# Row-sum reciprocals through a small DRAM tile, the first residual's constant folded, and the key stacking begun by ScalarE

## What is computed

```
x = L0(x)   1x1 conv to q, k, v (128 channels); per channel softmax(q k^T) v over the 32 x 32 image;
            1x1 conv back; y * inv + (beta - mean * inv); + x
x = L1(x)   group norm (32 groups); qkv; 8 heads of 32 channels over 1024 tokens:
            softmax(q^T k) v; projection + b_proj; + x
x = L2(x)   group norm (16); k, v; softmax of k over channels and over tokens; context = k v^T;
            out = context^T q; group norm; exact gelu; 1x1 conv; + the normalised input
x = L3(x)   + bias; separable FIR up by 2; leaky relu * sqrt 2; separable FIR down by 2
```

## Time and profile before

| what | us |
|---|---|
| median of 3 runs (lowest, highest) | 4347.69 (4339.87, 4350.91) |
| the profiled execution | 4343.08 |
| its span, first to last instruction | 4341.1 |
| TensorE (PE) busy | 3821.6 |
| VectorE (DVE) busy | 2956.3 |
| ScalarE (ACT) busy | 2988.7 |
| GpSimd (POOL) busy | 41.4 |

### The profile page before, as it was taken

The page is one execution under the profiler, slowest core; times in us unless marked ns, Lnnn a source line. Parts: engine busy times, 40 slices in busy tenths (PEclk is TensorE's granted clock), DMA queues, the critical chain, the costliest instruction groups (busy, mean ns, idle before and its releaser), DMA issues.

```text
span 4341.1 us, 73525 instructions
## 1 busy us (share of the span) xinstructions
PE 3821.6 (88%) x22913; PEld 1888.4 (44%) x22913; DVE 2956.3 (68%) x5147; ACT 2988.7 (69%) x6992; POOL 41.4 (1%) x57
## 2 busy tenths in 40 slices
PE   4989899898988989898898988989898998989876
PEld 2445445353453535445353443535445353444422
DVE  3666767677767776677677767767676677767653
ACT  1877677777777777667777767777667777767831
POOL 0000000000000000000000000000000000000000
PEclk7889999999999999999999999999999999989886
DMA  2111120111111011120111112011121111211000
GB/s 68 49 30 50 30 60 8 42 42 35 55 31 50 11 35 55 30 60 18 39 35 35 55 30 60 2 40 50 30 60 27 29 35 35 55 30 49 1 10 10
DMA packets 65221, 160.17 MB, mean 37 GB/s; under 512 B 15088, under 2 KB 16752, under 8 KB 62736
## 3 DMA queue, kind: packets, MB, share of 16 engines
q1 hardware_dynamic: 64784, 154.71, 13.5%
HBM read 19.91 MB, written 16.78 MB: 8 GB/s over the span
## 4 chain that ended last, share of the span: by engine, by line
PE 56%; DVE 17%; issue 14%; ACT 11%; SPq 1%; DVEq 1%; ACTq 0%; DMA 0%; POOL 0%; POOLq 0%
PE ps L1056 21%; PE ps L1129 8%; PE ps L1084 7%; PE ps L1100 7%; DVE mxh L640 6%; ACT ps L950 4%; PE ps L1518 3%; ACT prob L941 2%; DVE st L525 2%; PE ps L1550 2%; PE ps L1568 2%; PE ps L1577 1%; ACT u L1012 1%; PE ps L1116 1%; PE ps L1465 1%
## 5 line engine op out<-in xcount | busy, mean ns | idle before, releaser
L950 ACT ACTIVATE ps<-ps,mxh 128x512 f32<-128x512 f32 x2048 | 1369.8, 678 | 467.5 <-DVE mxh L640 441.2
L640 DVE TENSOR_REDUCE mxh<-ps 128x1 f32<-128x512 f32 x2048 | 1311.9, 681 | 343.7 <-PE ps L1100 335.7
L941 ACT ACTIVATE prob<-ps 128x512 f32<-128x512 f32 x2048 | 1128.1, 615 | 510.8 <-PE ps L1084 507.6
L1084 PE MATMUL ps<-qs,ks 97*128 97x512 f32 x2048 | 920.1, 528 | 90.5 <-ACT prob L941 63.3
L1100 PE MATMUL ps<-ks,qs 96*128 96x512 f32 x2048 | 740.2, 431 | 109.2 <-ACT ps L950 87.5
L1084 PEld LDWEIGHTS ps<-qs,ks 97*128 97x128 f32 x2048 | 365.8, 198 | 600.1 <-issue 372.1
L1129 PE MATMUL ps<-prob,vo 128*32 128x512 f32 x4096 | 584.0, 644 | 0.0
L1100 PEld LDWEIGHTS ps<-ks,qs 96*128 96x128 f32 x2048 | 411.6, 201 | 293.2 <-ACT ps L950 188.5
L950 ACT ACTIVATION_READ_ACCUMULATOR ps<-ps,mxh 128x1 f32 x2048 | 448.9, 219 | 0.0
L1056 PE MATMUL ps<-xn,wqk 128*128 128x512 f32 x512 | 266.8, 652 | 3.7 <-DVE xn L564 3.7
L1056 PE MATMUL ps<-wkv,xn 128*128 128x512 f32 x512 | 242.7, 608 | 19.3 <-DVE xn L564 18.4
(11 more groups left out here) (123 smaller groups left out, 3868.8 us busy)
## 6 DMA issues: line engine op xcount, KB each, us to landing
qs<-hi SPq DMA_DIRECT2D x256, 128.0 KB, 2.3
ks<-hi SPq DMA_DIRECT2D x256, 128.0 KB, 2.3
xb<-in_x SPq DMA_DIRECT2D x32, 512.0 KB, 4.2
qs<-lo SPq DMA_DIRECT2D x128, 128.0 KB, 2.3
ks<-lo SPq DMA_DIRECT2D x128, 128.0 KB, 2.3
xa<-xb SPq DMA_DIRECT2D x16, 1024.0 KB, 4.7
out<-xn SPq DMA_DIRECT2D x32, 512.0 KB, 2.6
qs<-mrow SPq DMA_DIRECT2D x64, 8.0 KB, 1.8
```

Source lines behind the costliest of these rows:

```text
L640: dve.tensor_reduce(mxh[:, k, e:e + 1], ps[:, MAX_BANKS[at % 3], :], AX_X, ALU.max, negate=True).then_inc(max_ok.sem, 1)
L941: act.activation(prob[:, n % 2, h, :], ps[:, k % 2, :], ACT.Exp).then_inc(p_ok.sem, 1)
L950: act.activation(ps[:, bank, :], ps[:, bank, :], ACT.Exp, bias=mxh[:, k, e:e + 1], accum_out=sumh[:, m // NT % 2, k, e:e + 1]).then_inc(su ...
L1084: pe.matmul(ps[:, k % 2, :], ks[0:STACK + 1, (u // 2) * Q4 + h, s * P:(s + 1) * P], qs[0:STACK + 1, u, h, :], start=True, stop=True).then_ ...
```

## The change

Three parts. First, `spread`, `pick`, `mrow` and `reciprocals_in` on VectorE go. VectorE copies only the 32 rows to `srow`; SyncE sends the lower 16 rows to a DRAM tile of 4 x 512 floats (in the slot of `turnN`, ahead of `rows_in`, which now reads srow) and, in the slot of `rowsN`, reads it back with a broadcast of each head's row to 32 partitions, into `recs`. Before it overwrites srow, VectorE waits for the store of the unit before and for the `normalise` before that. Second, xb keeps L0's residual without its constant; the mean of L1's first norm gets `add0` added before the averaging and subtracted again for the bias, and `b_proj` takes it up for the later residual. Third, the 12 transfers of each key stack are issued by ScalarE, behind its sums in the slots of v0a (ahead of gelu) and v1a; the query stacks stay with SyncE at q0b and q1b. `BANK` and `bank_free` are written anew for the entries that are left.

```diff
@@ SyncE
-            def stack(b, before, g, part):
+            def stack(b, before, g):
-                sp.wait_ge(hi1_ok.sem, hi1_ok(b, 2 * (2 * g + part + 1)))
-                sp.wait_ge(lo1_ok.sem, lo1_ok(b, 2 * (2 * g + part + 1)))
+                sp.wait_ge(hi1_ok.sem, hi1_ok(b, 4 * g + 2))
+                sp.wait_ge(lo1_ok.sem, lo1_ok(b, 4 * g + 2))
...
+            def reciprocals_out(b, t):
+                sp.wait_ge(row_ok.sem, row_ok(b, t + 1))
+                sp.wait_ge(recs_in.sem, recs_in(b, t - 1))
+                sp.dma_start(recd.rearrange("h (t n) -> (h t) n", n=P), srow[4 * Q4:8 * Q4, :])\
+                    .then_inc(recd_in.sem, 16)
+            def reciprocals_in(b, t):
+                sp.wait_ge(recd_in.sem, recd_in(b, t))
+                sp.dma_start(recs[:, :], recd.unsqueeze(1).to_broadcast([Q4, DH, HALF])).then_inc(recs_in.sem, 16)
@@ VectorE
+                if n == 0:
+                    step(dve.tensor_tensor(mv[:, n, :, 0], mv[:, n, :, 0], add0[:, :], ALU.add))
+                    last()
...
+                if n == 0:
+                    step(dve.tensor_tensor(gm[:, n, :, 0], gm[:, n, :, 0], add0[:, :], ALU.subtract))
+                    last()
...
-                if hf == 1:
-                    dve.wait_ge(res0.sem, res0(j, 2 * ct + 2))
-                    dve.tensor_scalar(xb[:, ct, :], xb[:, ct, :], add0[:, ct:ct + 1], None, ALU.add).then_inc(x1_ok.sem, 1)
...
+                if t:
+                    dve.wait_ge(recd_in.sem, recd_in(b, t - 1))
+                    dve.wait_ge(att_ok.sem, att_ok(b, t - 1))
                 bank = BANK[f"turn{t}"] if t else 6
-                dve.tensor_copy(mrow[:, :], ps[0:4 * Q4, bank, 0:P]).then_inc(row_ok.sem, 1)
                 dve.tensor_copy(srow[:, :], ps[0:8 * Q4, bank, 0:P]).then_inc(row_ok.sem, 1)
-            def reciprocals_in(b, u):
-                dve.wait_ge(spread_mm.sem, spread_mm(b, u + 1))
-                dve.wait_ge(att_ok.sem, att_ok(b, u))
-                dve.tensor_copy(recs[:, :], ps[:, BANK[f"rows{u + 1}"], :]).then_inc(spread_ok.sem, 1)
@@ ScalarE
+            def stack_keys(b, before, g):
+                act.wait_ge(lo1_ok.sem, lo1_ok(b, 4 * g + 4))
+                act.wait_ge(hi1_ok.sem, hi1_ok(b, 4 * g + 4))
+                if before is not None:
+                    act.wait_ge(s_mm.sem, s_mm(before, STEPS * Q4 // 2 * (g + 1)))
+                for h in range(Q4):
+                    for r, of in enumerate((hi1, hi1, lo1)):
+                        act.dma_start(ks[DH * r:DH * r + DH, g * Q4 + h, :].bitcast(F32),
+                                      of[DH * h:DH * h + DH, 1, :].bitcast(F32)).then_inc(stack_ok[g].sem, 16)
...
+                if name == "v0a":
+                    stack_keys(j, b, 0)
+                elif name == "v1a":
+                    stack_keys(b, i, 1)
@@ TensorE
-            def spread(b, t):
-                pe.wait_ge(row_ok.sem, row_ok(b, 2 * t + 2))
-                for a in range(4):
-                    ins = pe.matmul(ps[:, BANK[f"rows{t}"], a * P:(a + 1) * P], pick[:, a, :], srow[:, :],
-                                    start=True, stop=True)
-                ins.then_inc(spread_mm.sem, 1)
...
                 elif name == "wu00":
...
-                        pe.wait_ge(spread_ok.sem, spread_ok(b, 3))
+                        pe.wait_ge(row_ok.sem, row_ok(b, 4))
```

More of the change, by code:

```diff
@@ L114, in number, with chain_kernel @@
     return image[0] + image[1] if isinstance(image, tuple) else image
-def chain_kernel(nc, x, weights, vectors, rows, filters, consts, out):
+def chain_kernel(nc, x, weights, vectors, rows, filters, consts, recd, out):
     with ExitStack() as ctx:
@@ L257, in chain_kernel @@
         res0 = signal("res0", 4)
-        x1_ok = signal("x1_ok", 2)
-        gn_v = [signal(f"gn_v{n}", 12) for n in range(3)]
+        gn_v = [signal(f"gn_v{n}", 14 if n == 0 else 12) for n in range(3)]
         gn_mm = [signal(f"gn_mm{n}", 1) for n in range(3)]
@@ L385, in stack @@
                 for h in range(Q4):
[L386 to L395, removed]
+                    for r, of in enumerate((hi1, lo1, hi1)):
+                        sp.dma_start(qs[DH * r:DH * r + DH, 2 * g:2 * g + 2, h, :].bitcast(F32),
+                                     of[DH * h:DH * h + DH, 0, :].bitcast(F32).rearrange("p (a n) -> p a n", a=2))\
+                          .then_inc(stack_ok[g].sem, 16)
             def rows_in(b, u):
-                sp.wait_ge(row_ok.sem, row_ok(b, 2 * u + 1))
-                sp.dma_start(qs[STACK:STACK + 1, u % UNITS, :, :].bitcast(F32), mrow[:, :].bitcast(F32))\
+                sp.wait_ge(row_ok.sem, row_ok(b, u + 1))
+                sp.dma_start(qs[STACK:STACK + 1, u % UNITS, :, :].bitcast(F32), srow[0:4 * Q4, :])\
                     .then_inc(row_in.sem, 16)
+            def reciprocals_out(b, t):
[6 more added lines that the diff above has]
+                sp.dma_start(recs[:, :], recd.unsqueeze(1).to_broadcast([Q4, DH, HALF])).then_inc(recs_in.sem, 16)
             def store(i, ct):
@@ L409, in side @@
                     copy_x(b, i, j)
[L410 to L413, removed]
+                elif name == "q1b":
+                    stack(b, i, 1)
+                elif name == "q0b":
+                    stack(j, b, 0)
                 elif name in ("wd0b", "wd1b"):
@@ L417, in side @@
                     t = int(name[4])
+                    reciprocals_out(b, t)
                     if t < UNITS or j is not None:
                         rows_in(b, t)
+                elif name.startswith("rows"):
+                    reciprocals_in(b, int(name[4]))
             def first():
@@ L540, in variances @@
             def variances(n, i):
-                step, last = stepper(n, i, 5)
+                step, last = stepper(n, i, 6 if n == 0 else 5)
                 dve.wait_ge(gn_mm[n].sem, gn_mm[n](i, 1))
@@ L551, in factors @@
             def factors(n, i, scale, bias):
-                step, last = stepper(n, i, 9)
+                step, last = stepper(n, i, 10 if n == 0 else 9)
                 dve.wait_ge(gn_p[n].sem, gn_p[n](i, 1))
@@ L798, in side @@
                         sums_joined(b, digit)
-                elif name.startswith("rows"):
-                    reciprocals_in(b, digit - 1)
                 elif name in ("flipq", "flipk", "flipv"):
@@ L815, in side @@
                 elif name in ("stats1a", "stats1b"):
-                    dve.wait_ge(x1_ok.sem, x1_ok(j, part + 1))
+                    dve.wait_ge(res0.sem, res0(j, 2 * part + 2))
                     stats(0, j, xb, part)
@@ L1202, in bank_free @@
                     pe.wait_ge(kv_ok.sem, kv_ok(i, 14))
-                elif name == "rows1":
-                    pe.wait_ge(row_ok.sem, row_ok(b, 4))
                 elif name == "l0qa":
+                    if b is None:
+                        pass
+                    else:
+                        pe.wait_ge(row_ok.sem, row_ok(b, 2))
+                elif name == "l0qb":
                     if b is None:
@@ L1368, in bank_free @@
                     pe.wait_ge(zs_ok.sem, zs_ok(i, 3))
-                elif name == "rows3":
-                    pe.wait_ge(row_ok.sem, row_ok(b, 8))
                 elif name == "wu00":
@@ L1587, in side @@
                     turn(b, digit, digit < UNITS or j is not None)
-                elif name.startswith("rows"):
-                    spread(b, digit)
                 elif name.startswith("l0"):
@@ L1726 @@
     arrays["ident"] = np.eye(P, dtype=np.float32)
-    arrays["pick"] = np.zeros((2, Q4, 4, 4, Q4, DH), np.float32)
-    for h in range(Q4):
-        for t in range(4):
-            arrays["pick"][1, h, t, t, h] = 1.0
-    arrays["pick"] = arrays["pick"].reshape(8 * Q4, 4, P)
     for name, size in (("avg8", 8), ("avg16", 16)):
@@ L1739 @@
     out = nc.dram_tensor("out", (B, C, N), F32, kind="ExternalOutput").ap()
-    chain_kernel(nc, ap["x"], ap, ap["vectors"], ap["rows"], ap, ap, out)
+    recd = nc.dram_tensor("recd", (Q4, HALF), F32, kind="Internal").ap()
+    chain_kernel(nc, ap["x"], ap, ap["vectors"], ap["rows"], ap, ap, recd, out)
     got = run_bass_kernel_spmd(nc, [{"in_" + k: t for k, t in arrays.items()}], core_ids=[0])
```

76 lines of the change are left out of this document (36 added, 40 removed), and 13 rows, old and new, of the table BANK.

## The result

| kernel | median us of the runs (lowest, highest) | span of the profiled execution | mean granted clock |
|---|---|---|---|
| before | 4347.74 (4339.87, 4350.91) | 4341.1 | 0.931 |
| changed | 4487.27 (4483.99, 4487.48) | 4485.2 | 0.916 |

The ratio is 1.0322, with a 95% interval of 1.0304 to 1.034: the change makes the kernel slower by 140 us. The prediction said 4480.

A forecast was written before the change was run, and what follows sets the result against it. TensorE, busy 88% of the span, was taken to bound the kernel. From the profiled 4343 us, gains of 70, 12, 7 and 3 and losses of 113 and 114 gave 4478, stated as 4480; range 4350 to 4550.

The forecast's parts named there:

- ScalarE's queue is held by its issues: Behind v0a and v1a, 12 key issues each hold ScalarE's queue throughout, 7.55 us per row of twelve.
- Group 0, slot 41: ScalarE's issues delay its Gelu and exponential, adding 7.55 us to TensorE's existing gap in 15 images: 113 us.
- Group 1, slot 6: Issues delay slot 7's exponentials: 5.5 us net stall plus about 1.6 for low clock, 7.1 us in 16 images: 114 us.
- Spread: Removing the spread matmuls frees TensorE of 1.09 us in each of 64 units: 70 us.
- Slots 46 to 48: At rows3 the wide product no longer waits for the recs copy: 1.92 us instead of 1.09, 12 us more over 15 images.
- The fold: Ahead of the statistics, VectorE's second pass gives way to two small operations: 0.43 us an image, 7 us gained.
- The DRAM round trip hidden: Before normalise, the store and broadcast read take 7 us with a wait, within 8.8 us of cover: no cost.
- rival C: The DRAM round trip is late for VectorE: 11 us more, 4490; its chance is counted within the forecast's 0.64.
- Rival D: In dense slots 14 to 21 ScalarE takes TensorE's freed time, losing half of the 70 us: 4515; chance 0.06.
- The start: In the prologue, query and key stacks now overlap but share engines: 3 us gained.
- Rival A: ScalarE issues beside its work, so only the gains are left: about 4255 us, not slower; chance 0.14.
- Rival B: ScalarE's issues cost more than SyncE's, 0.80 us each, 9.6 for 12: 64 us more, 4545; chance 0.10.

The follow-up runs named there:

- e8: Changed kernel with its 24 ScalarE key issues an image spread over several slots, three at a time and once six; 4274.58 us, ratio 0.9842.
- e5: Kernel of e1 with only group 0's key transfers issued by ScalarE, behind v0a; 4326.09 us, ratio 0.9956.
- e10: Changed kernel with SyncE's 1 MB copy of xb to xa held back until group 1's key stack has landed; 4455.17 us, ratio 1.0255.
- e1: Changed kernel with the key stacks issued by SyncE again, the DRAM round trip and the fold kept; 4219.42 us, ratio 0.9705.
- e9: Kernel of e1 with four unread matmuls of the size of spread put back in each rowsN slot; 4293.98 us, ratio 0.9876.
- e6: Kernel of e1 with only group 1's key transfers issued by ScalarE, behind v1a; 4382.53 us, ratio 1.0082.
- e4: Kernel before with only the residual's constant folded into the mean and b_proj; 4343.6 us, ratio 0.9995.
- e11: Kernel of e1 with the constant's fold undone, leaving the DRAM round trip alone, in its second run; 4254.94 us, ratio 0.9792.

## Why the prediction was right, point by point

The sign and the mechanism hold, and the total lies 7 us from the forecast. That closeness is luck: the terms were off by about 40 us one way and 35 the other, and these errors cancelled.

- **ScalarE's queue is held by its issues: right.** 0.61 us each, priced at 0.63 (7.55 over 12). The Trainium skill, "Perfetto Trace Analysis", section "Summary: the profiler window per engine type", counts lock wait, descriptor generation and push as such a slice; the runs agree in that each issue starts only when the one before has ended, and e8 adds that compute already handed over runs on meanwhile. The Trainium skill, "DMA: Bandwidth & Descriptors", section "Issuing engines are not separate DMA queues", has the initiating time "usually small relative to the DMA itself"; here it is 0.61 us of a median 3.3 from issue to landing, and 24 of them an image cost 268 us.
- **Group 0, slot 41: right.** Predicted 7.55 an image, the table shows 7.19 in slot 42 and 0.41 in 43, over 15 images 114 us for 113. That e5's whole time shows 107 is partly luck (see there).
- **Group 1, slot 6: mis-sized.** The step 7.55 - 1.1 = 6.5 us took the time from a stretch with SyncE's queue alone at work. It asked what each moved transfer passes in ScalarE's order, and not what SyncE's queue, free earlier, would start beside it: the xa copy, which lengthens the last three issues by 1.6 us. Slots 7 and 8 grow by 8.8 us for 7.1; with the copy held back (e10) they grow by 7.5 against e1. TensorE's wait is 7.44 us for 6.5; the 0.98 of the earlier trace rows is gone, as foreseen. The stretch of slower clock behind the gap was foreseen too: the window shows 0.50, and the rest of the 8.8, 2.3 us, stands for the 1.6 priced.
- **Spread: right at 1.09 us for slots 14 and 62** (1.08 and 1.17).
- **Slots 46 to 48: mis-sized.** Priced at 1.92 us, it is 3.85 by the table's medians and 3.5 on the mean of 15 images, 52 us for 29. The prediction took the matmuls and part of the wait for the recs copy alone. Of the 52 us, 36 fall in slot 46 and 16 in 47 and 48, where the clock stands at 1.00 instead of the mean 0.73, which the prediction had at nothing. The idle time of TensorE ahead of these slots is shorter (0.90 us for 1.61); in e9, with the matmuls, it is gone and slots 47 and 48 are the same, so it is not the matmuls that decide here. Whether the gap brings the low clock was not tried by itself.
- **Slot 30: right on the mean, but unsteady.** Priced 1.09; over 15 images it is 1.16 us shorter in e1 and 1.01 in the changed kernel, while the medians of the table say 2.26 and 0.86. It is 2.5 us in 14 of 15 images of e5 and in none of e6 (3.5 to 4.1). The long value goes with the low clock, as the windows of e1 show; what sets it off is not shown.
- **The fold: 7 us priced;** slot 36 is 0.59 us shorter in every kernel that has it, 9 to 10 us, though alone (e4) the other slots take that back. Slots 38 and 39 are 0.85 us longer in the changed kernel, 12 us over 15 images that no step of the prediction had; 0.65 of it stands in e11 too, without the fold, so it goes with the DRAM part, and its cause was not tried.
- **The DRAM round trip hidden: right.** Rows of the product that reads recs, of the changed kernel: ns min/median/max, and the idle time for the read in us and times.

```profile
L687 DVE TENSOR_TENSOR att<-ps,recs x64: 653/679/693, 187.7 to 4326.5; 128x512 f32<-128x512 f32 x64
...
  DMA recs<-recd: 0.7, 1
```

  It waited once in 64 times. So rival C is out: the store lands in 1.3 us where I took 2.6. Rival D is out as well: slots 15 to 22 are unchanged, and slot 14 keeps its gain.
- **The start: 3 us priced,** about 10 measured. The wait of the earlier trace rows, 20.5 us in two pieces, is now one. The first piece stands before the first image's maxima and is 2.8 us shorter, with both queues issuing at once; the other, 7.0 us in slot 44 of the first image, is gone:

```profile
PE ps L1119 <- DMA ks<-lo: 10.7, 1, 10.7
```

- **Rival A, issues beside work:** refuted for twelve in a row, half right for three (e8). The prediction gave the break-even of a shorter hold, but no reason for one: it is the batch that decides. (That break-even is also slightly off: 31 H - 33.6 = 92 gives H = 4.1 us, where the prediction has 3.9.) **Rival B** came true in one place, by 1.6 us for group 1, and for a cause that it named and then argued away (the transfers of both queues meeting): I looked at the query stack and not at the 1 MB copy.

What the sum is with the measured terms, from the timelines of TensorE over images 0 to 14, with the price for as many images in brackets: slots 7 and 8 +133 us (107), 42 and 43 +114 (113), 46 to 48 -52 (-29), 14, 30 and 62 -49 (-49), slot 36 -10 (-6), slots 38 and 39 +12 (0), slot 44 of the first image -7 (in the 3 of the start), all others +4 (0); together 145. The first logits start 4 us earlier (131.43 for 135.42), the last image takes 6 us more to its last slot and the end 3 less. That is 144, the difference of the spans.

**What stays open.** TensorE's low-clock stretches of slots 0, 23, 30, 43 and 47 to 51 come and go from image to image and from version to version, and what sets off each is not shown; e5 and e6 show only that slot 30 changes with an edit over ten slots away. With it stay open why the fold is worth 27 to 36 us on top of the DRAM part and nothing alone, and some 20 us each in e6, e8 and e9. Nor is it shown why a 1 MB copy lengthens ScalarE's issues where other transfers, with the DMA engines as busy, do not.

## What to carry to other kernels

A DMA started by a compute engine costs that engine its issue time, 0.6 us for these, once the issues outlast the compute already handed over; price it by the batch, put it where the engine has idle time in the same slot, and spread it: the same 24 issues cost 268 us as two rows of twelve, and 55 us as six threes and one row of six. A queue that becomes free earlier starts its next transfer earlier, so look at what will then run beside the moved one. Where slots take several values from image to image, compare sums over all images, and not a median of a few. A short copy of another engine between TensorE and its next matmul can be worth more than the matmuls it serves, and the lower clock that goes with its gap has to be counted too.

## What the runs showed of the hardware that was not expected

- ScalarE's queue runs ahead of its engine: an issue that stands behind two activations in the program started 0.24 us before the first of them (1392.50 and 1392.74 in e8).
- An issue on one queue can be lengthened by another queue's copy: 1.86 us for two and 1.61 for one behind the issue of a 1 MB copy, and 0.61 each with the copy held back (e10). The DMA share does not tell the cases apart: at 1.07 in group 0 the issues took 0.61 to 0.63.
- An 8 KB store to DRAM lands in 1.3 us, under the 1.8 of the transfer of 8 KB from mrow to the query stack.
- The parts' effects do not add up, and most of what does not add up lies in slots where the granted clock comes and goes: parts that win 127 us together (e1) give 93 to 101 and 4 alone, and the keys' move costs 220 us alone and 268 with them.
